# A transformer block on one core: the second quad's queries between the first maxima, the max rows ahead of the third landing, biases in other periods, and pair 61's averages in another PSUM bank

## The chip, the cores and the metric

The kernel runs on one core of a Trainium2 chip. The metric is the device time of one execution in microseconds. Engines are called by the names that the profile uses: PE (TensorE, with PEld for its weight loads), DVE (VectorE), ACT (ScalarE), POOL (GpSimd), SP (the engine whose queue issues most of the DMAs). PSUM has eight banks of 128 partitions by 512 fp32 values, numbered 0 to 7 here.

## The reference, cut to what matters

Four batches of 512 tokens with 256 features pass one block: self-attention, cross-attention to a context of 512 rows with 192 features, and an MLP. Both attentions have 16 heads of 64 features with rotary positions.

```python
attn_in = _adaln(x, cond, ln1_w, ln1_b, g1_w, g1_b, b1_w, b1_b)
x = _attn(attn_in, attn_in, sa_wq, sa_wkv, sa_wo, sa_bo) + x
cross_in = _adaln(x, cond, ln1_w, ln1_b, g1_w, g1_b, b1_w, b1_b)
ctx_n = _ln(context, ca_lnc_w, ca_lnc_b)
x = _attn(cross_in, ctx_n, ca_wq, ca_wkv, ca_wo, ca_bo) + x
ffn_in = _adaln(x, cond, ln2_w, ln2_b, g2_w, g2_b, b2_w, b2_b)
h = jax.nn.gelu(ffn_in @ ff_w1 + ff_b1, approximate=False)
x = h @ ff_w2 + ff_b2 + x
```

`_attn` projects q, k and v, rotates q and k, takes softmax(q k^T / 8), averages v with it and projects the result with `wo`, plus a bias `bo`.

## The kernel before

**Precision.** Each fp32 operand of a large matmul is split into a high part (rounded) and a low part (the rest), and three products are summed: high by high, high by low, low by high (`parts`, L712). The high parts are made on ACT, the low parts by a subtraction on DVE or POOL (`low_qk` L1081, `low_o` L1077, `norm_split` L288, `low_weights` L296, `split_ffw` L1112).

**Units of work.** A pair is two heads of one batch, one in each half of the 128 partitions; there are 64 pairs (`PAIRS`), numbered g. Two neighbouring pairs are a quad (32 of them, `QUADS`, numbered u), which share weights and projections. A job j is one projection for a quad: job 2u gives the keys and job 2u+1 the queries (`k = 1 - j % 2`). A job's two halves e come out of PE (`project`), are multiplied with the rotation table on DVE (`rotate` L1086), added up on POOL (`rotate` L422) and moved by two DMAs of SP into `lo` (`land` L338). ACT rounds them into `hi` (`high_qk`), DVE subtracts (`low_qk`).

**The loop.** After a hand-written head, every engine runs `period(p)` for p = 0 to 63, in its own order, and then a tail with the MLP. In period p PE does, alternating, `score(p, i)` and `peak(p+1, i)` for i = 0 to 3, then `total(p-1)`, `average(p, kt)`, a norm's transposes if one is due, `project(p+4)`, and in every second period v's projection or the output projection. A peak is a trial product of high parts, from which DVE takes the negated maxima (`peak` L1061, `neg_max`); SP brings these as rows into `max_rows` (`land_max` L347), and `score` adds them through a matmul with `pick` before ACT takes the exponential (`exp`). POOL adds the four blocks of probabilities in three additions of 128x1024 (`add_probs`), which `total` sums over partitions. ACT and DVE make the inverse of that sum (`guess_inverse`, `normalise`), and DVE scales the average with it.

**What orders the work around the change.**

- Each engine does its instructions in program order and waits on counting semaphores. SP's queue is in order too.
- The head on PE ends with `peak(0, 0..3)`, `norm(2, ..)` and `project(3)`, the queries of quad 1. Each half of `project(3)` waits for a half of job 2's rotation, and its second half for maximum 2 of pair 0.
- `score(g, 0)` waits for `qk_low`, `max_landed`, `av_kept` (ACT has copied the last averages out of bank 1) and `o_low`. The scores use banks 0 to 3, the peaks banks 4 to 7. `peak(p+1, 0)` waits for both halves of job p+3's rotation on DVE (`roped`), and `peak(g, i)` for i above 1 waits for the maximum two before it.
- `peak(p+1, 0)` and `(.., 1)` also wait in `side_free` for the output projection's two sums, which DVE adds to x (`add_out` L1102) at the end of an even period.
- `sum_ps(60)` is bank 4, `sum_ps(63)` bank 6, all others bank 0. Averages are in bank 1.
- `low_qk` for pair 1 is on DVE in period 0. `low_qk(p+2)` comes before the rotation in most periods, and after it where DVE takes a norm's statistics (`stats_in`: periods 0, 5, 9, 13, 17 and some later ones).
- POOL adds the attention's output bias to x (`add_bias`, one 128x1024 addition per batch) in periods 0, 1, 5 and 7 for the first sublayer.
- In the tail, `hidden(f)` is the MLP's first matmul for block f. Block 0 uses bank 3 and block 1 bank 0, so `hidden(1)` waits for `o_low` 63, the `low_o` of pair 62.

## Time and profile before

| what | value |
|---|---|
| time, median of 3 runs | 1118.84 us (1118.40 to 1119.14) |
| the profiled execution's own time | 1118.88 us |
| its span | 1117.1 us, 18312 instructions |
| PE busy | 1097.2 us, 98% of the span |
| DVE busy | 858.1 us, 77% |
| POOL busy | 775.7 us, 69% |
| ACT busy | 636.9 us, 57% |
| mean granted PE clock | 0.994 of full |

The times of rows are us from the start of the span. A line of the timeline gives start, duration, engine, line of the kernel, operation, output and inputs, and in brackets the idle time of the engine before it and what ended that. Matmuls overlap, so a matmul's own duration is longer than the distance to the next. In a line with several instructions (x2, x4) the duration reaches from the first's start to the last's end.

### The profile page before, as it was taken

To read this page: it belongs to the slowest core of one execution; us is meant where nothing else is said; L and a number is where in the kernel's file an instruction comes from. 1 tells how busy PE (TensorE), PEld (TensorE's weight loads), DVE (VectorE), ACT (ScalarE), POOL (GpSimd) and SP (SyncE) were. 2 spreads that over 40 slices of the span, in tenths; PEclk is the share of its full clock that TensorE was granted. 3 is DMA by queue.
4 is the path that set the end of the run, shared out by engine and by line. 5 is a ranking of instruction groups with operands and counts; after the bars stand their busy time and mean duration, and the time that the engine had idled before them with its cause. 6 is when DMAs were issued, how large, how long until landed. Compare 5 with 4: busy or idle time off the path is not lost.

```text
span 1117.1 us, 18312 instructions
## 1 busy us (share of the span) xinstructions
PE 1097.2 (98%) x6904; PEld 785.1 (70%) x6904; DVE 858.1 (77%) x1023; ACT 636.9 (57%) x895; POOL 775.7 (69%) x503
## 2 busy tenths in 40 slices
PE   8989999999999999999999999999999999989998
PEld 7657666776666776666766667766666776756997
DVE  5878887878787777878888777777877777788554
ACT  6465565665666555577665555555555545775521
POOL 2687887787788767789799766777777667755210
PEclk9899999999999999999999999999999999999999
DMA  6312121311231111211121112211121111300001
GB/s 175 86 46 57 32 53 39 89 30 30 53 77 38 39 36 23 72 39 39 29 63 38 39 39 59 51 23 36 38 72 39 37 31 30 114 1 1 20 19 38
DMA packets 59606, 52.31 MB, mean 47 GB/s; under 512 B 23040, under 2 KB 42496, under 8 KB 59264
## 3 DMA queue, kind: packets, MB, share of 16 engines
q1 hardware_dynamic: 57632, 49.57, 18.5%
q10 hardware_dynamic: 1888, 1.59, 0.5%
q8 instruction: 55, 0.90, 0.3%
q14 instruction: 31, 0.25, 0.1%
HBM read 15.22 MB, written 2.10 MB: 16 GB/s over the span
## 4 chain that ended last, share of the span: by engine, by line
PE 90%; DVE 5%; ACT 2%; issue 1%; DMA 1%; SPq 0%; POOL 0%; ACTq 0%; POOLq 0%; DVEq 0%
PE ps L872 18%; PE ps L713 12%; PE ps L715 11%; PE ps L714 11%; PE ps L813 6%; PE ps L860 6%; PE ps L848 5%; PE ps L819 5%; PE ps L815 5%; PE ps L817 5%; PE ps L963 4%; DVE lo L1083 1%; PE ps L729 1%; DMA x<-x_dram 1%; DVE w_lo L1117 1%
## 5 line engine op out<-in xcount | busy, mean ns | idle before, releaser
L548 ACT ACTIVATE probs<-ps 128x1024 f32<-128x1024 f32 x256 | 262.5, 1027 | 208.0 <-PE ps L819 183.6
L1065 DVE TENSOR_REDUCE neg_max<-ps 128x2 f32<-128x1024 f32 x256 | 301.6, 1226 | 76.7 <-PE ps L848 76.7
L420 POOL TENSOR_TENSOR acc<-acc,probs 128x1024 f32<-128x1024 f32 x128 | 306.2, 2392 | 18.6 <-POOL acc L415 0.4
L872 PE MATMUL ps<-probs,v 128*64 128x512 f32 x1024 | 230.7, 592 | 0.0
L415 POOL TENSOR_TENSOR acc<-probs 128x1024 f32<-128x1024 f32 x64 | 153.2, 2394 | 72.1 <-ACT probs L548 72.1
L872 PEld LDWEIGHTS ps<-probs,v 128*64 128x64 f32 x1024 | 73.9, 137 | 146.1 <-issue 146.1
L429 POOL TENSOR_TENSOR eo<-tmp 128x512 f32<-128x512 f32 x63 | 89.7, 1424 | 120.2 <-DVE tmp L1092 120.1
L1092 DVE TENSOR_TENSOR tmp<-ps,rope 128x1024 f32<-128x1024 f32 x126 | 148.2, 1211 | 4.5 <-PE ps L715 4.3
L813 PE MATMUL ps<-max_rows,pick 64*128 64x512 f32 x512 | 109.3, 419 | 2.6 <-DVE o_lo L1079 1.6
L713 PE MATMUL ps<-xn_hi,w_hi 128*128 128x512 f32 x256 | 107.8, 421 | 2.5 <-DVE o_lo L1079 1.3
L848 PE MATMUL ps<-hi 64*128 64x512 f32 x512 | 104.8, 400 | 5.4 <-DVE neg_max L1065 2.6
L819 PE MATMUL ps<-hi,lo 64*128 64x512 f32 x512 | 104.0, 396 | 0.0
L715 PE MATMUL ps<-xn_hi,w_lo 128*128 128x512 f32 x256 | 102.8, 402 | 0.0
L815 PE MATMUL ps<-hi 64*128 64x512 f32 x512 | 102.7, 392 | 0.0
L817 PE MATMUL ps<-lo,hi 64*128 64x512 f32 x512 | 102.4, 390 | 0.0
L714 PE MATMUL ps<-xn_lo,w_hi 128*128 128x512 f32 x256 | 102.0, 398 | 0.0
L1083 DVE TENSOR_TENSOR lo<-lo,hi 128x1024 fp32r<-128x1024 f32 x64 | 98.3, 1535 | 0.0
L1070 DVE SCALAR_TENSOR_TENSOR ps<-ps,inv 128x512 f32<-128x512 f32 x64 | 44.8, 700 | 68.6 <-ACT inv L556 68.6
L580 ACT COPY v<-ps 128x512 f32<-128x512 f32 x64 | 37.4, 589 | 100.5 <-PE ps L715 100.5
L848 PEld LDWEIGHTS ps<-hi 64*128 64x128 f32 x512 | 81.0, 306 | 17.8 <-issue 5.2
L430 POOL TENSOR_TENSOR eo<-tmp 128x512 f32<-128x512 f32 x63 | 81.3, 1291 | 0.0
L713 PEld LDWEIGHTS ps<-xn_hi,w_hi 128*128 128x128 f32 x256 | 49.0, 192 | 45.4 <-issue 33.9
(116 smaller groups left out, 2250.0 us busy)
## 6 DMA issues: line engine op xcount, KB each, us to landing
lo<-eo SPq DMA_DIRECT2D x126, 256.0 KB, 3.2
w_raw<-pack_dram SPq DMA_DIRECT2D x16, 192.0 KB, 3.9
x<-x_dram SPq DMA_DIRECT2D x4, 512.0 KB, 7.5
w_raw<-pack_dram SPq DMA_DIRECT2D x8, 256.0 KB, 4.3
max_rows<-neg_max SPq DMA_DIRECT2D x128, 2.0 KB, 2.0
w_raw<-w_dram SPq DMA_DIRECT2D x2, 1024.0 KB, 5.8
out<-x SPq DMA_DIRECT2D x8, 256.0 KB, 2.2
ctx_in<-ctx_dram SPq DMA_DIRECT2D x4, 384.0 KB, 4.2
```

The lines of the kernel that those rows point to most:

```text
L420: pool.tensor_tensor(acc[:, g % 2, :, :], acc[:, g % 2, :, :], probs[:, i, :, :], ALU.add).then_inc(added, 1)
L548: act.activation(probs[:, i, :, :], score_ps(i), ACT.Exp, scale=SCALE).then_inc(exped, 1)
L713: pe.matmul(out, a_hi, b_hi, start=first, stop=False)
L714: pe.matmul(out, a_hi, b_lo, start=False, stop=False)
L715: return pe.matmul(out, a_lo, b_hi, start=False, stop=last)
L813: pe.matmul(out[:, h, :], pick[half[h], :], max_rows[half[h], :], start=True, stop=False)
L815: pe.matmul(out[:, h, :], k_hi[half[h], cut], q_hi[half[h], :], start=False, stop=False)
L817: pe.matmul(out[:, h, :], k_hi[half[h], cut], q_lo[half[h], :], start=False, stop=False)
L819: mm = pe.matmul(out[:, h, :], k_lo[half[h], cut], q_hi[half[h], :], start=False, stop=True)
L848: mm = pe.matmul(out[:, h, :], hi[half, g % 2, 0, cut], hi[half, g % 2, 1, :], start=True, stop=True)
L872: mm = pe.matmul(av_ps[DH * h:DH * h + DH, :], v[:, u % 2, kt, c:c + DH], probs[:, kt, h, :], start=(kt == 0), stop=(kt == TT - 1))
L1065: dve.tensor_reduce(neg_max[:, g % 2, :, i], peak_ps(i), AX.X, ALU.max, negate=True).then_inc(maxed, 1)
```

## The change

- **Head, PE.** `project(3)` is cut in four steps of three matmuls, `project_3(e, kt)`: (0,0) before `peak(0, 2)`, (0,1) before `peak(0, 3)`, (1,0) and (1,1) after it, all before `norm(2, ..)`. The waits for job 2's rotation are left out, that for maximum 2 stays.
- **Head, SP.** `land_max(0)` comes ahead of `land(2)`.
- **Head, ACT and POOL.** `high_qk(1)` comes ahead of `guess_rstd(2)`. The low parts of pair 1 are made on POOL after `rotate(3)`, with a semaphore of their own, and no more on DVE in period 0. DVE has nothing then between the maxima of pair 1 and the statistics of norm 3.
- **Biases.** The first sublayer's four `add_bias` go to periods 13, 15, 18 and 21 and wait for the output projection of quad 4 + b; `add_out` no longer waits for them in that sublayer's first two rounds.
- **Pair 61.** Its averages go to bank 5. `score(62, 0)` then waits neither for `av_kept` nor for `o_low`; `peak(63, 0)` waits for both.
- **Periods 61 to 63, DVE.** In period 61 the statistics of norm 13 come ahead of `normalise(60)`, and their means ahead of `low_o(60)`. `split_ffw` is one subtraction of 128x2048 instead of four of 128x512, twice. In period 63 DVE adds probability blocks 2 and 3 of pair 63 into `tmp`, POOL only blocks 0 and 1, and `total(63)` sums both with four matmuls instead of two.

```diff
-        av_ps = ps[:, 1, :]
+        def av_ps(g):
+            return ps[:, 5 if g == PAIRS - 3 else 1, :]
...
-        bias_in.update({0: 0, 1: 1, 5: 2, 7: 3})
+        bias_in.update({13: 0, 15: 1, 18: 2, 21: 3})
...
             land(1)
+            land_max(0)
             land(2)
-            land_max(0)
             load_x(3)
...
                 pool.wait_ge(ln_rows, TT * (n + 1))
+                if sublayer == 0:
+                    pool.wait_ge(o_added, 2 * (NB + b) + 2)
...
                     add_probs(p, 1)
-                    add_probs(p, 2)
-                    add_probs(p, 3)
+                    if p < PAIRS - 1:
+                        add_probs(p, 2)
+                        add_probs(p, 3)
...
             rotate(3)
+            pool.wait_ge(qk_high, 2)
+            pool.tensor_tensor(lo[:, 1, :, :], raw_qk[:, 1, :, :], hi[:, 1, :, :], ALU.subtract).then_inc(qk_low_1, 1)
...
             high_qk(0)
+            high_qk(1)
             guess_rstd(2)
-            high_qk(1)
             norm_rows(2)
...
+            def project_3(e, kt):
+                if e == 0 and kt == 0:
+                    pe.wait_ge(w_split, 2)
+                    pe.wait_ge(ln_split, 4)
+                if e == 1 and kt == 0:
+                    pe.wait_ge(maxed, 3)
+                c = slice(kt * 256 + e * 128, kt * 256 + (e + 1) * 128)
+                mm = parts(job_ps(3, e), w_hi[:, 0, c], w_lo[:, 0, c], xn_hi[:, 1, kt, :], xn_lo[:, 1, kt, :],
+                           kt == 0, kt == 1)
+                if kt == 1:
                     mm.then_inc(projected, 1)
...
                 if kt == 0:
-                    pe.wait_ge(qk_low, g + 1)
+                    if g == 1:
+                        pe.wait_ge(qk_low_1, 1)
+                    else:
+                        pe.wait_ge(qk_low, max(g, 1))
                     pe.wait_ge(max_landed, 32 * (g + 1))
-                    if g > 0:
+                    if g > 0 and g != PAIRS - 2:
                         pe.wait_ge(av_kept, g)
-                    if g > 1:
+                    if g > 1 and g != PAIRS - 2:
                         pe.wait_ge(o_low, g - 1)
...
                     if i == 0 and p == PAIRS - 2:
                         pe.wait_ge(o_low, PAIRS - 3)
+                        pe.wait_ge(av_kept, PAIRS - 2)
...
             def total(g):
-                pe.wait_ge(added, 3 * g + 3)
+                pe.wait_ge(added, 3 * g + (3 if g < PAIRS - 1 else 1))
...
                     pe.wait_ge(o_added, 2 * (QUADS - 1))
+                    pe.wait_ge(last_added, 1)
                 for h in range(2):
-                    mm = pe.matmul(sum_ps(g)[DH * h:DH * h + DH, :], ones[:, :], acc[:, g % 2, h, :], start=True, stop=True)
+                    out = sum_ps(g)[DH * h:DH * h + DH, :]
+                    mm = pe.matmul(out, ones[:, :], acc[:, g % 2, h, :], start=True, stop=g < PAIRS - 1)
+                    if g == PAIRS - 1:
+                        mm = pe.matmul(out, ones[:, :], tmp[:, 0, h, :], start=False, stop=True)
...
             modulate(3)
+            project_3(0, 0)
             peak(0, 2)
+            project_3(0, 1)
             peak(0, 3)
+            project_3(1, 0)
+            project_3(1, 1)
             norm(2, 0)
             norm(2, 1)
-            project(3)
...
             def add_out(u, r):
                 _, b, phase = quad(u)
-                if r == 0:
+                if r == 0 and u >= 2 * NB:
...
+            def split_ffw(m):
+                dve.wait_ge(ffw_high, 4 * m + 4)
                 high, low, raw = ((w1_hi, w1_lo, w1_raw), (w2_hi, w2_lo, w2_raw))[m]
...
+                dve.tensor_tensor(low[:, :, :], raw[:, :, :], high[:, :, :], ALU.subtract).then_inc(ffw_split, 1)
+
+            def add_last_probs():
+                dve.wait_ge(exped, 4 * PAIRS)
+                dve.tensor_tensor(tmp[:, 0, :, :], probs[:, 2, :, :], probs[:, 3, :, :], ALU.add).then_inc(last_added, 1)
...
-                if p == 0:
-                    low_qk(1)
+                if p == PAIRS - 3:
+                    norm_stats(stats_in[p])
                 if is_pair(p - 1):
                     normalise(p - 1)
-                if p in stats_in and p != PAIRS - 3:
-                    norm_stats(stats_in[p])
+                if p == PAIRS - 1:
+                    add_last_probs()
+                if p in stats_in:
+                    if p != PAIRS - 3:
+                        norm_stats(stats_in[p])
                     norm_means(stats_in[p])
                 if is_pair(p - 1):
                     low_o(p - 1)
-                if p == PAIRS - 3:
-                    norm_stats(stats_in[p])
-                    norm_means(stats_in[p])
                 if p == PAIRS - 2:
-                    for c in range(4):
-                        split_ffw(0, c)
+                    split_ffw(0)
```

## Rows read from the trace of the kernel before

**Rows 1.** Windows: stretch, busy us of each engine, PEclk, DMA share, GB/s.

```profile
36.00:43.00 7.00, 6.31 (x20) 5.25 (x20) 4.53 (x11) 3.43 (x6) 3.56 (x3) 0.53 0.47 113
...
105.00:980.00 875.00, 874.14 (x5595) 611.45 (x5595) 689.53 (x767) 515.29 (x708) 666.44 (x405) 1.00 0.20 46
...
1019.00:1022.00 3.00, 3.00 (x8) 2.33 (x8) 2.70 (x5) 2.71 (x5) 2.83 (x4) 0.50 0.01 3
```

**Rows 2.** Timeline of TensorE in the head and periods 0 and 1.

```profile
36.69 1.97 PE L729 MATMUL ps<-ident,z 128*128 128x128 f32 x8 [1.40 <-ACT z L505]
...
58.02 0.62 PE L848 MATMUL ps<-hi 64*128 64x512 f32 x2 [1.54 <-DVE tmp L1092]
...
62.43 0.63 PE L848 MATMUL ps<-hi 64*128 64x512 f32 x2 [1.70 <-DVE neg_max L1065]
...
64.99 1.80 PE L860 MATMUL ps<-acc,ones 128*64 128x512 f32 x4
```

**Rows 3.** Timeline of VectorE in the head and periods 0 and 1.

```profile
32.26 4.61 DVE L1065 TENSOR_REDUCE neg_max<-ps 128x2 f32<-128x1024 f32 x4
...
43.34 1.22 DVE L1092 TENSOR_TENSOR tmp<-ps,rope 128x1024 f32<-128x1024 f32 x1 [0.86 <-PE ps L715]
...
49.96 3.38 DVE L1083 TENSOR_TENSOR lo<-lo,hi 128x1024 fp32r<-128x1024 f32 x1
...
57.80 3.43 DVE L1083 TENSOR_TENSOR lo<-lo,hi 128x1024 fp32r<-128x1024 f32 x1
```

**Rows 4.** Timeline of GpSimd over the same stretch.

```profile
40.22 2.63 POOL L293 TENSOR_TENSOR xn_lo<-z,xn_hi 128x512 fp32r<-128x512 f32 x2 [3.24 <-ACT xn_hi L520]
...
45.90 1.29 POOL L430 TENSOR_TENSOR eo<-tmp 128x512 f32<-128x512 f32 x1
...
49.89 5.70 POOL L420 TENSOR_TENSOR acc<-acc,probs 128x1024 f32<-128x1024 f32 x2
...
57.77 2.39 POOL L437 TENSOR_TENSOR x<-x,bias_rows 128x1024 f32<-128x1024 f32 x1
```

**Rows 5.** Timeline of SyncE: DMA issues behind pair 0's maxima.

```profile
37.01 1.17 SPq L345 DMA_DIRECT2D lo<-eo  x2
38.30 1.77 SPq L354 DMA_DIRECT2D max_rows<-neg_max  x2
```

**Rows 6.** DMA issues of the page: size, median us from issue to landing.

```profile
lo<-eo SPq DMA_DIRECT2D x126, 256.0 KB, 3.2
...
max_rows<-neg_max SPq DMA_DIRECT2D x128, 2.0 KB, 2.0
```

**Rows 7.** Timeline of period 18 and its end: GpSimd, VectorE, TensorE.

```profile
328.59 4.91 POOL L420 TENSOR_TENSOR acc<-acc,probs 128x1024 f32<-128x1024 f32 x2
...
333.61 1.21 DVE L1083 TENSOR_TENSOR lo<-lo,hi 128x1024 fp32r<-128x1024 f32 x1
...
337.01 1.37 DVE L1109 TENSOR_TENSOR x<-ps,x 128x512 f32<-128x512 f32 x2
...
338.60 0.41 PE L848 MATMUL ps<-hi 64*128 64x512 f32 x2
```

**Rows 8.** Timeline of TensorE in period 3, behind its first score.

```profile
93.25 0.62 PE L848 MATMUL ps<-hi 64*128 64x512 f32 x2 [0.20 <-DVE x L1109]
```

**Rows 9.** Timeline of TensorE in periods 62 and 63 and the tail.

```profile
989.46 0.50 PE L813 MATMUL ps<-max_rows,pick 64*128 64x512 f32 x2 [1.55 <-DVE o_lo L1079]
...
995.26 1.08 PE L860 MATMUL ps<-acc,ones 128*64 128x512 f32 x4
...
1018.19 0.51 PE L713 MATMUL ps<-xn_hi,w_hi 128*128 128x512 f32 x1 [1.27 <-DVE o_lo L1079]
```

**Rows 10.** Timeline of VectorE and ScalarE in the same stretch.

```profile
989.23 1.40 DVE L1050 BATCH_NORM_STATS2 stats<-x 128x6 f32<-128x256 f32 x4
...
1004.90 8.64 DVE L1117 TENSOR_TENSOR w_lo<-w_raw,w_hi 128x512 fp32r<-128x512 f32 x4
...
1010.85 0.63 ACT L556 ACTIVATE inv<-inv 128x512 f32<-128x512 f32 x1
```

More of the change, by code:

```diff
@@ L742, in project @@
                 for e in range(2):
[L743 to L746 removed]
+                    if j == 1:
+                        pe.wait_ge(roped, e + 1)
                     for kt in range(KT):
@@ L1150, in period @@
                 if p == PAIRS - 2:
-                    for c in range(4):
-                        split_ffw(1, c)
+                    split_ffw(1)
             norm_stats(0)
```

21 lines of the change are left out of this document (7 added, 14 removed).

## The prediction, made before the change was run

> **What bounds the kernel.** I read the windows first, then the list of what TensorE waited for, then the timelines of the two places where it waits, and last the DMA issues. Between 105 and 980 us PE is busy for 874.1 of 875 us at full clock [rows 1], so nothing off PE can be worth a microsecond there. PE's idle time lies in the head with periods 0 and 1, and from period 60 on, and there it is a chain over the other engines that counts. In the head the reader should see three things: PE waits 1.40 us for the normalised rows and then runs at a granted clock of 0.53 from 36 to 43 us [rows 1, 2]; PE waits twice in period 1, 1.54 us for DVE's rotation and 1.70 us for a maximum [rows 2]; and before both waits DVE has a subtraction of 3.4 us in its queue [rows 3]. In the tail PE waits 1.55 us at 989.46 and 1.27 us at 1018.19, each time for a `low_o` of DVE [rows 9].
>
> **Why 3.4 us.** The same subtraction took 1.21 us in period 18 [rows 7]. The one at 57.80 began 0.03 us behind POOL's bias addition, which ended at 60.16; 1.07 us later DVE was done [rows 3, 4]. The one at 49.96 stands beside additions of POOL in the same way. So a DVE operation with both inputs in SBUF that comes behind a POOL operation waits for its end, then takes its own 1.1 to 1.2 us, and POOL's next one waits in turn.
>
> The Trainium skill ("SBUF — State Buffer", Who interferes with whom) says this as a rule: DVE with two SBUF inputs and a GpSimd instruction that reads SBUF share a port under an exclusive lock, and the second to issue blocks until the first is done. By that rule, the trace agrees: 3.43 us beside 1.21.
>
> **Head, step by step.** Pair 0's four maxima fill 32.26 to 36.87 on DVE, 1.15 us each [rows 3], so maximum 2 is there at 35.7. `project_3`'s first half (two steps of about 0.7 us at full clock) fits between the peaks without delaying a maximum. Its second half starts at 35.75 and ends at 37.2. `norm(2)` then starts 0.5 us later than its 36.69 [rows 2], and gives that back if the clock has stayed up (its eight transposes took 1.97 us at half clock).
>
> DVE ends the maxima at 36.87, then has `low_qk(0)` and `modulate(1)`, 2.5 us, then both halves of rotation 3 at 1.22 us each: 41.8 instead of 44.56 [rows 3]. POOL can't begin `rotate(3)` at 41.8, though. Its two splits of norm 2 ended at 42.85 [rows 4], and I put them between 42.4 and 43.4. `land(2)` is now behind `land_max(0)`: that one is issued at 36.95 and 37.5, its landing (2.0 us [rows 6]) is 39.5, and `land(2)` moves from 37.01 to 38.1 [rows 5], second half 38.7, landed with the usual 3.2 us at 41.9 and with 3.6 at 42.3 [rows 6]. So `rotate(3)` begins at 42.6, bounds 42.4 and 43.4, instead of 44.64.
>
> From there POOL is one chain: rotation 2.55 us to 45.15 (before: to 47.19 [rows 4]), the new subtraction of pair 1 at POOL's 2.4 us for 128x1024 [rows 4] to 47.6, and three additions at 2.4 us to 54.9. That is 0.7 us earlier than the 55.59 of before [rows 4], in spite of one more operation.
>
> The Trainium skill ("GPSIMD Engine Reference", Engine selection) speaks against this move: elementwise work on two inputs belongs on VectorE, GpSimd being about twice as slow. Here the rows are 2.39 against 1.21 us, so the move would cost 1.2 us of engine time; what it buys is that DVE loses 3.38 us.
>
> DVE meanwhile: the maxima of pair 1 begin when `peak(1, 0)` may run, at 41.85, and end at about 47.1. Norm 3's statistics follow at once. Rotation 4 is limited by PE's `project(4)` and ends at 53.2 instead of 57.88, so the wait of 1.54 us goes. Then `low_qk(2)` meets POOL's third addition, waits until 54.9, ends at 56.05; the first maximum of pair 2 is there at 57.2, and `peak(2, 2)` can start then. Before, it was 62.43 [rows 2]: 5.2 us earlier, and PE still waits there, about 1.4 us. From `peak(2, 2)` to `total(0)` it took 2.56 us and the sum's four matmuls 1.80 us [rows 2]; those four take 1.08 at full clock [rows 9]. With full clock `total(0)` is at 58.7, 6.3 us earlier; with a clock that falls again after the waits, 4.7 us. I can't tell which, since PE still has gaps of 1.3, 1.0 and 1.4 us in 38 to 57 us. **Term: -5.6 us**, bounds -6.3 and -3.9 (low clock and `rotate(3)` at 43.4). A low clock earlier, in period 0, costs nothing: POOL's chain does not wait for PE. `high_qk(1)` ahead of `guess_rstd(2)` fills 1.8 us in which ACT waits for the variances anyway: 0.
>
> **Biases.** Those of periods 0 and 1 were 2.4 us each in POOL's queue; period 0's is the one that held `low_qk(2)`, counted above. Without period 1's, POOL and DVE are earlier before period 3, where PE waited 0.20 us [rows 8]: -0.2 (0 to -0.5). Period 13 has the same neighbours as 5 (a norm's statistics, a weight split in the next period), 15 the same as 7; what they cost moves with them: 0, within 0.5 either way. Period 18 is different. It is even, with `add_out` at its end. POOL's additions end at 333.50 and the bias would start there; `low_qk` comes at 333.61 [rows 7]. It then waits 2.3 us and ends at 337.0 instead of 334.82. The first `add_out`, done at 337.7 before, comes to 339.9, and the peak that needs it started at 338.60 [rows 7]. **Term: +1.3 us**, bounds 0 (if DVE is first, by 0.1 us) and +2.2. Period 21 is odd: no `add_out`, 0.
>
> **Pair 61 and the statistics.** `score(62, 0)` loses its wait and starts at 987.9. `peak(63, 0)` then waits for `low_o(60)`, which ends where the statistics began, at 989.25 [rows 10]. The statistics now fill DVE's idle time before `normalise(60)`, so `low_qk(63)` (1.2 us) comes at once and the maxima of pair 63 start at 990.4. The first is there at 991.6, `peak(63, 2)` follows, and with one more score and peak `total(61)` starts at 993.15 instead of 995.26 [rows 9]. **Term: -2.1 us**, bounds -1.1 (the start of `peak(63, 0)` alone) and -2.3. All up to `total(62)` hangs on it.
>
> **Last splits.** The four subtractions at 1004.90 took 8.64 us beside POOL [rows 10]. One of 128x2048 takes about 2.3 us plus at most one POOL operation (1.3 us): DVE is free at 1006.5, and `normalise(62)` waits only for the inverse, 1011.48 [rows 10] less 2.1, so 1009.4, instead of 1013.5. Then come 2.2 us of `normalise`, 1.2 of the new addition, 1.4 of statistics [rows 10], 0.6 of means, 0.7 of `low_o`: `hidden(1)` can start at 1015.5 instead of 1018.19 [rows 9]. `total(63)` no longer waits for POOL; its two extra matmuls are in PE's wait before `hidden(1)`, 1.4 us long. **Term: -0.6 us** beyond the 2.1, bounds 0 and -0.9.
>
> **Clock in the tail.** From 1019 to 1022 the clock was 0.50 after two waits of PE close together [rows 1, 9]. It lost 1.5 us there. Now there is one wait. At 989.46 one wait of 1.55 us was not followed by a low clock. **Term: -0.8 us**, bounds 0 and -1.4 (then DVE's first hidden split holds PE). Behind it PE has no wait, so all of this reaches the end.
>
> **Sum.** -5.6 -0.2 +1.3 -2.1 -0.6 -0.8 = -8.0 us, from the profiled execution's 1118.88, which is the median of the runs to 0.04 us: 1110.9.
>
> **Rivals.**
> - *Late chain and low clock in the head* (POOL's splits end at 43.4, PE's clock falls after 57 us): head -3.9, no gain of clock in the tail, the rest as above: -5.5, 1113.4. For it: PE's gaps. Against: fewer of them than before. Chance 0.22.
> - *All terms at their good end*: DVE first in period 18, full clock: 1108.2. For it: a margin of 0.1 us. Chance 0.15.
> - *Biases block everywhere*: the 2.2 us of period 18 at the other three as well: +6.6, 1117.5, which is no change. Against: periods 5 and 7 had a bias and PE lost under 1 us in all of 105 to 980 [rows 1]. Chance 0.05.
> - *Slower*: after the shift POOL's third addition runs later against DVE, so that `low_qk` is held in every even period as before period 3. Its price there was 0.2 us of waiting [rows 8] and, by my estimate, 0.27 to fill the pipeline again; over 30 even periods 0.47 each is 14 us: 1125. It decides from 22 periods on. Against: POOL waits for DVE's rotation in each period and is set right by that. Chance 0.04.
>
> **Chances.** Forecast 0.50 (own range 1109.5 to 1112.5); rivals as given; 0.04 for other sums that are faster. A measurement of this kernel tells about 0.2%, 2.2 us, from no change. Faster 0.91, same 0.05, slower 0.04. The range 1108.4 to 1114.6 leaves out those two, a part of the good end and of the bad clock.
>
> **What the profile after would show.** `rotate(3)` of POOL starting at 42.6 and pair 1's subtraction at 45.2; `low_qk(2)` ending at 56; `peak(2, 2)` near 57.2 with a wait of 1.4 us; `total(0)` between 58.7 and 60.3; a wait of PE in period 19 of 1.3 us; `total(61)` 2.1 us sooner after `total(60)`; `hidden(1)` 2.7 us sooner, with one wait before it. The prediction is wrong if `land(2)` lands after 44 us, if `rotate(3)` waits for it, or if PE has new waits in the middle.

## The result and the profile after

The changed kernel took 1112.12 us in the median of 4 runs (1110.40 to 1112.95), the kernel before 1118.99 us in the same comparison (4 runs, 1118.40 to 1119.45). The ratio is 0.9937, 95% interval 0.9920 to 0.9954: faster by 0.6%. 1110.9 was forecast, in a range of 1108.4 to 1114.6. The profiled execution took 1110.40 us, with a span of 1108.6 us.

The page of the changed kernel (span, busy time of each engine with its share and its instructions):

```profile
span 1108.6 us, 18301 instructions
...
PE 1091.2 (98%) x6908; PEld 779.6 (70%) x6908; DVE 851.0 (77%) x1017; ACT 636.2 (57%) x895; POOL 775.2 (70%) x502
```

Windows of the changed kernel, with the columns of [rows 1]: the head, the middle, the end of the chain in the tail.

```profile
36.00:43.00 7.00, 4.57 (x32) 3.61 (x32) 6.17 (x13) 4.21 (x6) 3.63 (x4) 1.00 0.43 105
105.00:980.00 875.00, 872.80 (x5567) 608.79 (x5567) 690.95 (x769) 514.75 (x707) 670.07 (x405) 1.00 0.20 45
...
1012.00:1022.00 10.00, 9.87 (x64) 8.63 (x63) 9.11 (x15) 6.70 (x11) 5.02 (x4) 1.00 0.00 1
```

The granted clock, 0.53 in 36 to 43 us and 0.50 in 1019 to 1022 us before [rows 1], is 1.00 in both places. In the middle PE now idles 2.2 us instead of 0.9; 1.14 us of it is the wait at the end of period 18.

Timeline of TensorE in the head, answering to [rows 2]:

```profile
39.75 0.50 PE L836 MATMUL ps<-max_rows,pick 64*128 64x512 f32 x2 [1.55 <-DMA max_rows<-neg_max]
...
53.92 0.63 PE L872 MATMUL ps<-hi 64*128 64x512 f32 x2 [0.28 <-DVE tmp L1123]
...
57.30 0.62 PE L872 MATMUL ps<-hi 64*128 64x512 f32 x2 [0.66 <-DVE neg_max L1096]
...
59.03 1.08 PE L886 MATMUL ps<-acc,ones 128*64 128x512 f32 x4
```

Timeline of GpSimd and VectorE in the same stretch, answering to [rows 3, 4]: rotation 3, pair 1's subtraction, pair 0's three additions, the epsilon of norm 3 (`var_eps`), `low_qk(2)`.

```profile
42.73 1.30 POOL L433 TENSOR_TENSOR eo<-tmp 128x512 f32<-128x512 f32 x1 [0.35 <-DMA lo<-eo]
...
45.23 2.38 POOL L478 TENSOR_TENSOR lo<-lo,hi 128x1024 fp32r<-128x1024 f32 x1
...
47.55 2.38 POOL L419 TENSOR_TENSOR acc<-probs 128x1024 f32<-128x1024 f32 x1
...
48.95 1.02 DVE L1090 TENSOR_SCALAR var_eps<-mean_var 128x4 f32<-128x4 f32 x1
...
50.08 4.95 POOL L424 TENSOR_TENSOR acc<-acc,probs 128x1024 f32<-128x1024 f32 x2
...
53.69 2.43 DVE L1114 TENSOR_TENSOR lo<-lo,hi 128x1024 fp32r<-128x1024 f32 x1
```

The chain is the one forecast: POOL from `rotate(3)` on, `low_qk(2)` held until POOL's last addition ends at 55.03, then the first maximum, then `peak(2, 2)`. The line to notice is `var_eps`, an operation on 128x4 values. It takes 0.17 us when POOL is idle; here it takes 1.02 us, and ends 0.04 us behind POOL's addition (47.55 + 2.38 = 49.93). In this execution it costs nothing, for DVE waits for PE behind it.

Timeline of period 18 and its end, answering to [rows 7]:

```profile
325.98 2.40 POOL L443 TENSOR_TENSOR x<-x,bias_rows 128x1024 f32<-128x1024 f32 x1
...
326.16 3.30 DVE L1114 TENSOR_TENSOR lo<-lo,hi 128x1024 fp32r<-128x1024 f32 x1
...
331.65 1.27 DVE L1140 TENSOR_TENSOR x<-ps,x 128x512 f32<-128x512 f32 x2
...
332.47 0.62 PE L872 MATMUL ps<-hi 64*128 64x512 f32 x2 [1.14 <-DVE x L1140]
```

Timeline of periods 61 to 63, answering to [rows 9, 10]:

```profile
983.14 0.87 DVE L1090 TENSOR_SCALAR var_eps<-mean_var 128x4 f32<-128x4 f32 x1
...
983.92 0.68 DVE L1110 TENSOR_TENSOR o_lo<-ps,o_hi 128x512 fp32r<-128x512 f32 x1
...
984.70 0.63 PE L872 MATMUL ps<-hi 64*128 64x512 f32 x2 [0.81 <-DVE o_lo L1110]
...
988.75 1.08 PE L886 MATMUL ps<-acc,ones 128*64 128x512 f32 x4
...
1010.86 0.50 PE L722 MATMUL ps<-xn_hi,w_hi 128*128 128x512 f32 x1 [0.29 <-DVE o_lo L1110]
```

Here the same small operation does cost: it stands ahead of `low_o(60)` in DVE's queue, and it waits for POOL's addition, which ends at 983.98 (the two additions of pair 60 began at 979.09 and filled 4.89 us).

**Where the time went.** The table compares the starts of some matmuls of PE in the two profiles; `total(g)` stands for the first of its matmuls. `down(0)` is the first matmul of the second hidden layer; behind it PE has no wait.

| stretch | before | after | difference | forecast |
|---|---|---|---|---|
| start to `total(0)` | 64.99 | 59.03 | -5.96 | -5.6 |
| to `total(2)` | 32.33 | 30.99 | -1.34 | -0.2 |
| to `total(60)` | 886.07 | 888.23 | +2.16 | +1.3 |
| to `total(61)` | 11.87 | 10.50 | -1.37 | -2.1 |
| to `hidden(1)` | 22.93 | 22.11 | -0.82 | -0.6 |
| to `down(0)` | 5.85 | 4.60 | -1.25 | -0.8 |
| to the end | 93.06 | 93.14 | +0.08 | 0 |
| span | 1117.1 | 1108.6 | -8.5 | -8.0 |

**The spread of the runs.** The executions of one kernel differ by more than some of these rows. The kernel before took 1118.4 to 1119.5 us in all four executions of the first comparison. In later comparisons its executions lay in two heaps: of the 23 of the last comparison 18 took 1114.3 to 1116.0 us and 5 took 1119.1 to 1119.3 us. The changed kernel, run again, took 1112.42 us (7 runs, 1110.6 to 1115.8) beside 1115.70 of the kernel before, ratio 0.9965 (0.9949 to 0.9981). In the other comparisons some executions also lay at 1117.3 to 1118.9 us. So the table speaks for an execution of the upper heap; against the lower heap, as in the second comparison, the change is worth some 3 us. The experiments below come from four later comparisons. Their medians alone can seldom tell a microsecond; their traces can.

### The profile page after: what moved, and what is told of

Read it like the earlier page. It is cut to its first block, busy times and chain, and to the rows that moved or that the text cites. A ratio compares the mean times of both kernels' runs of the same rounds, so it can differ in the third digit from the quotient of the medians.

```text
span 1108.6 us, 18301 instructions
## 1 busy us (share of the span) xinstructions
PE 1091.2 (98%) x6908; PEld 779.6 (70%) x6908; DVE 851.0 (77%) x1017; ACT 636.2 (57%) x895; POOL 775.2 (70%) x502
## 4 chain that ended last, share of the span: by engine, by line
PE 91%; DVE 3%; ACT 2%; issue 1%; DMA 1%; POOL 1%; SPq 0%; ACTq 0%; POOLq 0%
PE ps L900 18%; PE ps L722 12%; PE ps L723 11%; PE ps L724 11%; PE ps L836 6%; PE ps L886 6%; PE ps L872 6%; PE ps L842 5%; PE ps L838 5%; PE ps L840 5%; PE ps L994 4%; PE ps L738 1%; DMA x<-x_dram 1%; DVE lo L1114 1%; DVE neg_max L1096 1%
## 5 line engine op out<-in xcount | busy, mean ns | idle before, releaser
L424 POOL TENSOR_TENSOR acc<-acc,probs 128x1024 f32<-128x1024 f32 x126 | 301.1, 2390 | 18.1
L1114 DVE TENSOR_TENSOR lo<-lo,hi 128x1024 fp32r<-128x1024 f32 x63 | 94.3, 1497 | 0.0
```

What stands on the lines that cost most here:

```text
L424: pool.tensor_tensor(acc[:, g % 2, :, :], acc[:, g % 2, :, :], probs[:, i, :, :], ALU.add).then_inc(added, 1)
```

## The experiments

### The changed kernel and the kernel before, once more

`after_again` is the changed kernel, `before_again` the kernel before; neither has an edit.

> The changed kernel itself, beside the others of this call. Theory 1: faster than the kernel before by 5 to 7 us in the median; the runs spread over some 2.5 us, because the clock falls at one place or another between 8 and 60 us, and a fall behind the maxima of period 0 costs 0.3 us at total(0), one in period 2 over 1 us. Rival: the gain is the same within 0.3 us in each run, and total(0) is at 59.0 us again.

> The kernel before, unchanged, profiled once more. Its executions on this chip lie in two heaps, near 1115.1 and near 1118.6 us, on the first chip at 1118.4 to 1119.5. Theory (the two heaps are one program with PE's clock low at different places of the head and the tail): if this execution is of the lower heap, total(0) starts 2 to 4 us before the 64.99 us of the first profile, with the clock low for less of 32 to 66 us, distances between totals from period 4 on agree within 0.1 us, and the rest of the difference is the tail's low clock in 1019 to 1022 us. If it is of the upper heap, all milestones agree with the first profile within 0.5 us. Rival (the middle differs: another pace of the periods, or of the DMA landings): total(0) agrees and the distances from period 4 on differ by 0.05 us or more each.

`after_again`: `total(0)` at 59.82 us and `total(2)` at 91.87 instead of 59.03 and 90.02. From `total(2)` to the end it took 1018.5 us against 1018.6. All of the 1.8 us between the two profiles of one kernel lie in the first 92 us. In 40 to 48 us the granted clock was 0.79 there instead of 1.00.

`before_again`: its profiled execution was of the upper heap (1119.13 us, span 1117.3), and the milestones agree with the first profile within 0.3 us (64.93, 97.27, 983.65, 995.52; the clock 0.50 in 36 to 40 us again). The ratio to the kernel before is 1.0001 (0.9986 to 1.0016), which is what this measurement makes of no change at all. No execution of the lower heap was profiled. The mean granted clock of the executions doesn't tell the heaps apart: in this comparison it was 0.991 to 0.994 in the upper one and 0.992 to 0.997 in the lower one. Whether the place of the low clock does is neither shown nor refuted.

### The biases back in periods 0, 1, 5 and 7

```diff
-        bias_in.update({13: 0, 15: 1, 18: 2, 21: 3})
+        bias_in.update({0: 0, 1: 1, 5: 2, 7: 3})
...
-                if sublayer == 0:
-                    pool.wait_ge(o_added, 2 * (NB + b) + 2)
...
-                if r == 0 and u >= 2 * NB:
+                if r == 0:
```

> All of the change, but the first sublayer's biases stay in periods 0, 1, 5 and 7. Theory 1 (my steps): the wait of 1.14 us in front of period 19's second peak goes and period 17-to-18's sum distance falls from 16.54 to 15.0 us; total(0) stays near 59.0 us, since low_qk(2) is behind POOL's third addition, ahead of the bias; period 1's bias gives back 0.6 us before period 3. Sum: 1 us faster than the changed kernel, 0.9 either way. Rival (the biases in periods 0 and 1 were what held the head): total(0) comes 2 us later and the whole is 1 to 3 us slower than the changed kernel.

Time 1111.42 us (6 runs, 1109.8 to 1113.2), ratio 0.9947 (0.9930 to 0.9964). `total(0)` came at 61.96, and not because of the bias. Timeline of GpSimd, VectorE and TensorE:

```profile
55.71 3.35 DVE L1112 TENSOR_TENSOR lo<-lo,hi 128x1024 fp32r<-128x1024 f32 x1
...
60.25 0.63 PE L870 MATMUL ps<-hi 64*128 64x512 f32 x2 [1.60 <-DVE neg_max L1094]
...
60.51 2.39 POOL L441 TENSOR_TENSOR x<-x,bias_rows 128x1024 f32<-128x1024 f32 x1
```

The bias runs at 60.51, behind the subtraction and the peak that it was said to hold. What made the head late is the clock, 0.50 in 36 to 40 us in this execution: POOL's rotation 3 began at 45.70 instead of 42.73, 2.97 us later, and `total(0)` 2.93 us later. In the new order of the head it is POOL's last addition that holds `low_qk(2)`, so moving the bias out of period 0 brings nothing at `total(0)`. From `total(0)` to `total(2)`, where period 1's bias is, it took 32.02 us and after the change 30.99. This need not be the bias: two executions of the changed kernel differ there by as much (30.99 and 32.05 us).

Elsewhere the biases did what was forecast, and a swap costs nothing: the distance from `total(5)` to `total(6)` is 15.90 with the bias in 5 and 15.49 without, from `total(13)` to `total(14)` 15.51 and 15.87. From `total(17)` to `total(18)` it is 15.02 with no bias in period 18 and 16.54 with one.

### The third bias in period 19

```diff
-        bias_in.update({13: 0, 15: 1, 18: 2, 21: 3})
+        bias_in.update({13: 0, 15: 1, 19: 2, 21: 3})
```

> All of the change, but the third batch's bias is added in period 19 instead of 18. Theory 1: low_qk of period 18 no longer stands behind the bias, the 1.14 us wait of PE goes and the distance of the sums falls from 16.54 to 15.0 us: 1.5 us faster than the changed kernel, nothing lost in period 19, whose low_qk comes before POOL's bias. Rival: POOL has additions, a weight split, the bias and a rotation in period 19, 14.7 us of a period of 15.1, and falls behind, so that the wait comes one period later with 0.5 us or more.

Time 1110.47 us (6 runs, 1108.8 to 1112.9) beside 1112.42 of the changed kernel in the same comparison; ratios 0.9946 (0.9929 to 0.9963) and 0.9965. The intervals overlap; the trace decides. Timeline of period 18 and of the bias in period 19:

```profile
326.29 1.22 DVE L1114 TENSOR_TENSOR lo<-lo,hi 128x1024 fp32r<-128x1024 f32 x1
...
329.68 1.38 DVE L1140 TENSOR_TENSOR x<-ps,x 128x512 f32<-128x512 f32 x2
...
343.52 2.40 POOL L443 TENSOR_TENSOR x<-x,bias_rows 128x1024 f32<-128x1024 f32 x1
```

The subtraction takes 1.22 us instead of 3.30, `add_out` begins 2 us sooner, and PE's wait is gone. `total(17)` to `total(18)` is 15.05 again, and `total(19)` to `total(20)` 15.31 instead of 15.05. From `total(2)` to `total(60)` it took 886.80 us, 1.4 less than after the change. The `low_qk` of period 19 began at 340.98, before the bias. Two kernels below have this edit too, with medians of 1110.24 and 1110.36 us. The three can't be told apart; their medians are the lowest of all.

### Pair 61's averages and the statistics as before

```diff
-            return ps[:, 5 if g == PAIRS - 3 else 1, :]
+            return ps[:, 1, :]
...
-                    if g > 0 and g != PAIRS - 2:
+                    if g > 0:
...
-                if p == PAIRS - 3:
-                    norm_stats(stats_in[p])
...
                     low_o(p - 1)
+                if p == PAIRS - 3:
+                    norm_stats(stats_in[p])
+                    norm_means(stats_in[p])
```

> All of the change, but pair 61's averages in bank 1 with the old waits of score(62), and norm 13's statistics and means behind low_o(60) as before. Theory 1: total(60) to total(61) goes back from 10.50 to 11.87 us, so 1.4 us slower than the changed kernel and nothing else moves. Rival (the tail is held by low parts and splits further on, so that this time is given back there): hidden(1) starts at the same distance from total(60) and the end moves by less than 0.4 us.

Time 1113.48 us (10 runs, 1112.3 to 1115.1), ratio 0.9969 (0.9958 to 0.9981), in one comparison with `bias_back` at 1111.42. From `total(60)` to `total(61)` it took 11.88 us, before 11.87, after 10.50. Timeline of VectorE and TensorE in period 61:

```profile
984.91 0.69 DVE L1110 TENSOR_TENSOR o_lo<-ps,o_hi 128x512 fp32r<-128x512 f32 x1 [0.65 <-ACT o_hi L583]
985.52 1.39 DVE L1081 BATCH_NORM_STATS2 stats<-x 128x6 f32<-128x256 f32 x4
...
985.75 0.50 PE L836 MATMUL ps<-max_rows,pick 64*128 64x512 f32 x2 [1.55 <-DVE o_lo L1110]
```

That is the wait of [rows 9] at its old length: taken out of the change, this part costs 1.38 us. The next experiment says why it isn't 2.1.

### Norm 13's means behind `low_o(60)`

The bias is in 19 here too.

```diff
-                if p in stats_in:
-                    if p != PAIRS - 3:
-                        norm_stats(stats_in[p])
+                if p in stats_in and p != PAIRS - 3:
+                    norm_stats(stats_in[p])
                     norm_means(stats_in[p])
...
                     low_o(p - 1)
+                if p == PAIRS - 3:
+                    norm_means(stats_in[p])
```

> The third bias in period 19 as before, and norm 13's aggregation and epsilon (128x2 and 128x4) behind low_o(60) instead of ahead of it. Theory (the part of the pair-61 term that did not come is the 128x4 operation of DVE, held 0.87 us behind POOL's addition, with low_o(60) behind it): low_o(60) can start at the end of ACT's o_hi, 4.2 us after total(60)'s four matmuls have ended instead of 4.6, so peak(63, 0) starts 0.4 to 0.5 us sooner after total(60), 6.0 instead of 6.45, and total(61) comes 0.3 to 0.5 us sooner, 10.0 to 10.2 us after total(60) instead of 10.50. Rival (ACT's exponential of (62, 0) stands behind the square root that needs the moved epsilon, and sets the pace then): peak(63, 0) sooner by as much, but the exponential of (62, 0) 0.5 us later, and total(61) 10.4 to 10.8 us after total(60). A third theory (what holds peak(63, 0) is not the lock): peak(63, 0) unmoved. The whole against the kernel with the bias in 19 alone: -0.4 us, within what a timing can tell: about 1110.

Time 1110.24 us (6 runs, 1109.4 to 1111.1), ratio 0.9948 (0.9932 to 0.9965). Timeline of period 61, all engines:

```profile
983.59 0.69 DVE L1110 TENSOR_TENSOR o_lo<-ps,o_hi 128x512 fp32r<-128x512 f32 x1 [0.65 <-ACT o_hi L583]
...
984.38 0.63 PE L872 MATMUL ps<-hi 64*128 64x512 f32 x2 [0.38 <-DVE o_lo L1110]
...
984.61 0.17 DVE L1090 TENSOR_SCALAR var_eps<-mean_var 128x4 f32<-128x4 f32 x1
...
985.16 1.92 ACT L557 ACTIVATE probs<-ps 128x1024 f32<-128x1024 f32 x2
...
986.21 0.19 PEld L836 LDWEIGHTS ps<-max_rows,pick 64*128 64x128 f32 x2 [0.35 <-ACT probs L557]
```

`low_o(60)` starts as soon as ACT has made its input. The epsilon takes 0.17 us, since POOL's addition ended at 984.08. `peak(63, 0)` starts 6.01 us after `total(60)` (978.37) instead of 6.45: the small operation held it for 0.44 us. `total(61)` gains 0.05 us of that (10.45 instead of 10.50), for ACT's square root waits for the moved epsilon, the exponential of (62, 0) starts 6.79 us after `total(60)` instead of 6.14, and PE waits for it. The rival was right: with the small operation no longer in front of `low_o(60)`, the stretch is bound by ACT.

### The last splits in four pieces again

```diff
-                dve.wait_ge(ffw_high, 4 * m + 4)
-                dve.tensor_tensor(low[:, :, :], raw[:, :, :], high[:, :, :], ALU.subtract).then_inc(ffw_split, 1)
...
+                for c in range(4):
+                    cut = slice(c * N, (c + 1) * N)
+                    dve.wait_ge(ffw_high, 4 * m + c + 1)
+                    dve.tensor_tensor(flat[1][:, cut], flat[2][:, cut], flat[0][:, cut], ALU.subtract)\
+                       .then_inc(ffw_split, 1)
```

> All of the change, but the MLP weights' low parts are four subtractions of 128x512 each time, as before. Theory 1: they alternate with POOL's operations and end near 1006 us instead of 1001.4, so normalise(62) starts up to 1 us behind its inverse, hidden(1) comes up to 1 us later and the end as much. Rival (POOL has so much less in period 63 that four pieces fit as well): normalise(62) starts with its inverse at the same distance from total(62), and the time is the same within 0.3 us.

Time 1111.61 us (5 runs, 1110.4 to 1113.1), ratio 0.9955 (0.9938 to 0.9973). Timeline of VectorE:

```profile
998.85 6.47 DVE L1149 TENSOR_TENSOR w_lo<-w_raw,w_hi 128x512 fp32r<-128x512 f32 x4
1005.45 0.70 DVE L1101 SCALAR_TENSOR_TENSOR ps<-ps,inv 128x512 f32<-128x512 f32 x1
```

The four pieces take 6.47 us (one piece took 3.00 in the changed kernel), and still end 0.13 us before `normalise(62)`, for which ACT's inverse is ready then. From `total(61)` to `hidden(1)` it took 22.10 us, in the changed kernel 22.11, and the rest of the span agrees as well. The rival was right. Making one subtraction of the four brings nothing, given the other edits.

### Pair 63's additions on POOL again

```diff
-                    if p < PAIRS - 1:
-                        add_probs(p, 2)
-                        add_probs(p, 3)
+                    add_probs(p, 2)
+                    add_probs(p, 3)
...
-                    if g == PAIRS - 1:
-                        mm = pe.matmul(out, ones[:, :], tmp[:, 0, h, :], start=False, stop=True)
...
-                if p == PAIRS - 1:
-                    add_last_probs()
```

> All of the change, but the last pair's blocks 2 and 3 are added on POOL again, and total(63) has two matmuls. Theory 1: total(63) waits for POOL's third addition until 1.2 us after hidden(0), but low_o(62) is 1.1 us sooner, so hidden(1) starts at the same distance from total(62) within 0.3 us; the end moves by less than 0.5 us unless the clock falls behind the two waits, which then costs 1.3 us. Rival (the move of the addition is what took the tail's second wait away): hidden(1) 1 us or more later.

Time 1112.65 us (7 runs, 1112.0 to 1113.8), ratio 0.9966 (0.9953 to 0.9979). Timeline of VectorE and TensorE:

```profile
1010.75 0.98 DVE L1086 TENSOR_SCALAR var_eps<-mean_var 128x4 f32<-128x4 f32 x1
1011.64 0.68 DVE L1106 TENSOR_TENSOR o_lo<-ps,o_hi 128x512 fp32r<-128x512 f32 x1
...
1011.76 1.08 PE L884 MATMUL ps<-acc,ones 128*64 128x512 f32 x4 [1.22 <-POOL acc L424]
```

`total(63)` comes 7.34 us after `total(62)` instead of 6.03. Most of that is given back, since there are two matmuls less and the addition is gone from DVE's queue: `hidden(1)` comes 22.19 us after `total(61)` instead of 22.11. From there to `down(0)` it takes 4.94 us instead of 4.60, with a wait of 0.48 us for the first hidden split. So this part is worth 0.4 us, 0.1 ahead of `hidden(1)` and 0.3 behind it. Here, too, the small operation is held until POOL's addition ends, with a `low_o` behind it.

### Pair 1's subtraction on DVE again

```diff
-            pool.wait_ge(qk_high, 2)
-            pool.tensor_tensor(lo[:, 1, :, :], raw_qk[:, 1, :, :], hi[:, 1, :, :], ALU.subtract).then_inc(qk_low_1, 1)
...
+                if p == 0:
+                    dve.wait_ge(qk_high, 2)
+                    dve.tensor_tensor(lo[:, 1, :, :], raw_qk[:, 1, :, :], hi[:, 1, :, :], ALU.subtract)\
+                       .then_inc(qk_low_1, 1)
```

This was run once with the bias in 18 (`low1_on_dve`) and once with it in 19 (`low1_bias19`).

> All of the change, but pair 1's low parts are subtracted on DVE in period 0 again, not on POOL. Theory 1: POOL's chain starts its additions 2.4 us sooner (45.2), the third ends near 53.6 with one wait for DVE; DVE's subtraction costs 1.2 to 1.7 us that lie in its wait for project(4); low_qk(2) starts at 53.7 free of POOL, so peak(2, 2) is near 56.1 instead of 57.3: the move to POOL brings nothing or costs 1 us, and the gain of the head is project_3's alone. Rival (the move off DVE is the head's gain, as the prediction's text weighs it: DVE loses 3.4 us): rotation 4 and the maxima of pair 2 are late again, total(0) is 2 to 3 us later and the kernel as much slower than the changed one.

> Pair 1's subtraction on DVE again, ahead of low_qk(2) in period 0, and the third bias in period 19. Theory (a subtraction of DVE that stands alone costs DVE 1.2 us, and POOL's chain of rotation, subtraction and three additions loses 2.4 us of its length, but DVE's subtraction falls beside an addition and is held to its end, so that nothing is won): total(0) at 60.1 to 60.4 us with the clock falling after 42 us, 59.0 to 59.6 without; behind period 0 all distances as with the bias in 19. Time 1110.5 to 1111.5. Rival (POOL's shorter chain is worth what the prediction took from its length, 1.2 us or more): total(0) at 58 us or sooner, time 1109.5 or less.

Times 1112.56 us (6 runs), ratio 0.9959 (0.9944 to 0.9973), and 1110.36 us (6 runs, 1109.5 to 1112.7), ratio 0.9954 (0.9936 to 0.9972). Timeline of the first, GpSimd and VectorE:

```profile
47.97 5.71 POOL L424 TENSOR_TENSOR acc<-acc,probs 128x1024 f32<-128x1024 f32 x2
...
48.95 2.47 DVE L1157 TENSOR_TENSOR lo<-lo,hi 128x1024 fp32r<-128x1024 f32 x1
```

DVE's subtraction is held to the end of an addition and takes 2.47 us; POOL's next addition waits in turn, so that POOL loses 0.8 us of the 2.4 that it saves (5.71 for two additions instead of 4.9). `total(0)` came at 60.15 and 61.48 us, but the clock was low in both, the second at 0.65 already in 32 to 36 us, ahead of the edit. So neither can be laid beside the changed kernel's first profile. The first of them can be laid beside the four profiles that have the subtraction on POOL and the same clock, 0.79 in 40 to 48 us: their `total(0)` is at 59.30 to 59.84, 0.3 to 0.9 us sooner. But its `total(2)`, at 91.14, is sooner than theirs (91.46 to 91.87), and the second median, 1110.36, is close to 1110.24, that of the kernel with the means behind, in the same comparison. Whether the move to POOL gains anything in the time stays open.

### `project_3` behind the peaks, and the rows behind the third landing

```diff
-            project_3(0, 0)
             peak(0, 2)
-            project_3(0, 1)
             peak(0, 3)
-            project_3(1, 0)
-            project_3(1, 1)
             norm(2, 0)
             norm(2, 1)
+            project_3(0, 0)
+            project_3(0, 1)
+            project_3(1, 0)
+            project_3(1, 1)
```

```diff
-            land_max(0)
             land(2)
+            land_max(0)
```

> All of the change, but project_3's four steps stand behind norm(2) as before. Theory 1: rotation 3 ends on DVE at 44.6 again, POOL's rotate(3) runs at 44.6 instead of 42.7 and its chain with the new subtraction ends 1.9 us later, so total(0) is 2 us later, and 1 to 2 us more if the clock falls as it did from 36 to 43 us: 2 to 4 us slower than the changed kernel. Rival (the queue of DVE and POOL in period 0 sets total(0) whatever the projection does): less than 1 us slower.

> The rows of maxima are again issued behind the third landing; the rest is the changed kernel. The part alone. Theory (the head is POOL's chain from rotate(3) on, which waits for this landing): land(2) is issued at 37.0 instead of 38.26, so rotate(3) of POOL starts when its own splits have ended, 42.4 us, 0.35 sooner; score(0, 0) waits for the rows, which land at 40.5 to 41 instead of 39.6, so it starts 1.2 us later; the maxima of pair 1 begin up to 1 us later, and total(0) is within 0.4 us of 59.0 where the clock is the same. Rival (score(0, 0) sets the head): total(0) 1 us or more later. Clock rival: PE's longer wait ahead of score(0, 0) brings a low clock in 36 to 48 us, and total(0) comes at 60 or later.

`project3_behind`: 1112.23 us (5 runs), ratio 0.9958 (0.9943 to 0.9973). PE waits again for the normalised rows and its clock falls to 0.50 in 36 to 40 us, as before the change; DVE's rotation 3 begins at 41.74 us instead of 39.36, and the chain follows it:

```profile
37.18 1.97 PE L738 MATMUL ps<-ident,z 128*128 128x128 f32 x8 [1.24 <-ACT z L514]
...
44.76 1.29 POOL L433 TENSOR_TENSOR eo<-tmp 128x512 f32<-128x512 f32 x1 [1.42 <-DVE tmp L1123]
```

`rotate(3)` at 44.76 instead of 42.73 and `total(0)` at 61.05 instead of 59.03: both 2.0 us later. By the profiles this is the largest single part of the head, the low clock included. The timed runs don't show it: 1112.23 us is no more than the 1112.42 of the changed kernel in another comparison.

`maxrows_behind`: 1111.53 us (7 runs, 1110.6 to 1111.8), ratio 0.9957 (0.9940 to 0.9973), in one comparison with two kernels of 1110.3 that have the bias in 19. The landing no longer holds POOL, and PE waits 3.39 us for the rows:

```profile
41.57 0.50 PE L836 MATMUL ps<-max_rows,pick 64*128 64x512 f32 x2 [3.39 <-DMA max_rows<-neg_max]
...
42.32 1.29 POOL L433 TENSOR_TENSOR eo<-tmp 128x512 f32<-128x512 f32 x1
```

`rotate(3)` is 0.4 us sooner, `score(0, 0)` 1.8 us later, the clock falls to 0.86 in 40 to 44 us and 0.71 in 44 to 48 us, and `total(0)` comes at 60.09, 1.06 us later. POOL's chain is not what made it late, for its last addition ends 0.45 us sooner than after the change, and `low_qk(2)` (55.80) takes 1.22 us, unheld: it stands behind rotation 4, and that behind PE. These are the clock rival's numbers. How much of it is the clock and how much the later `score(0, 0)` isn't separated.

## Why the forecast came out right, and what it had wrong

**Head, -5.6, measured -5.96: right step by step in the profiled execution, but for two.** `rotate(3)` was put at 42.6 us and came at 42.73, but for another reason than the one forecast. The landing was counted at 41.9 to 42.3, ahead of the end of POOL's splits. The splits ended at 42.37 and POOL then waited 0.35 us for the landing, which the prediction had named as a sign of being wrong. The other is the sum itself: with a low clock `peak(2, 2)` at 57.2 and the old 2.56 us behind it give 59.76, 5.2 us earlier, not 4.7.

The other steps: pair 1's subtraction was put at 45.2 and came at 45.23. `low_qk(2)` ends: 56.05, came at 56.12. `peak(2, 2)`: 57.2, came at 57.30. `total(0)`: 58.7 to 60.3, came at 59.03. One detail was off: PE's wait ahead of `peak(2, 2)` was 0.66 us and not 1.4, because PE itself had waited 0.28 us for rotation 4 and issued `peak(2, 0)` only at 53.92. The rotation of job 4 stood behind the held `var_eps`, but not because of it: it waited 1.18 us more for PE. The clock, said to be unknowable, stayed at 1.00 in this execution.

Of the 5.96 us the reversals above account, by profiles whose clock differs, for 2.0 (`project_3`) and 1.1 (the order of the landings); `high_qk(1)` ahead of `guess_rstd(2)` was not taken back in any run, and how the rest divides isn't shown. In the three profiles with full clock from 32 to 48 us (the changed kernel, the bias in 19, the splits in four) `total(0)` starts at 58.98 to 59.16; in the other four with the same head, all at a lower clock in 40 to 48 us, at 59.30 to 59.84.

**A low clock early in period 0, put at nothing.** "POOL's chain does not wait for PE" is true, but at the low clock another chain is the longer one: PE, pair 1's maxima, norm 3's statistics and epsilon, rotation 4. Timeline of GpSimd and VectorE in the kernel with pair 61 as before, at a clock of 0.68 in 40 to 44 us:

```profile
50.22 4.93 POOL L424 TENSOR_TENSOR acc<-acc,probs 128x1024 f32<-128x1024 f32 x2
...
50.26 2.37 DVE L1090 TENSOR_SCALAR var_eps<-mean_var 128x4 f32<-128x4 f32 x1
52.54 2.54 DVE L1123 TENSOR_TENSOR tmp<-ps,rope 128x1024 f32<-128x1024 f32 x2
55.00 1.23 DVE L1114 TENSOR_TENSOR lo<-lo,hi 128x1024 fp32r<-128x1024 f32 x1
```

The epsilon comes 1.3 us later than in the changed kernel's first profile, meets the next addition of POOL and is held for 2.37 us; rotation 4 follows without a wait, and `low_qk(2)` is not held at all. In two others rotation 4 also waits 0.2 us for PE. In all four profiles `low_qk(2)` takes 1.21 to 1.25 us and starts at 55.00 to 55.56, instead of 53.69, held, for 2.43.

**To `total(2)`, -0.2, measured -1.34: two things were left out.** The first 0.72 us lies between `total(0)` and `total(1)` and is the clock. Before, it was at 0.50 until 66.5 us, past the start of `total(0)`: its four matmuls took 1.80 us [rows 2] and now take 1.08. The prediction quoted both numbers, but measured its gain at the start of `total(0)` and so left the difference out. The other 0.62 us lies between `total(1)` and `total(2)`. The term counted POOL and DVE "earlier before period 3, where PE waited 0.20 us". What happens there is a race of two operations. Timeline of the kernel before, of the changed kernel and of the kernel with the means behind, in period 2:

```profile
87.55 2.69 DVE L1083 TENSOR_TENSOR lo<-lo,hi 128x1024 fp32r<-128x1024 f32 x1
```

```profile
78.39 5.96 POOL L424 TENSOR_TENSOR acc<-acc,probs 128x1024 f32<-128x1024 f32 x2
...
80.87 1.22 DVE L1114 TENSOR_TENSOR lo<-lo,hi 128x1024 fp32r<-128x1024 f32 x1
```

```profile
78.40 4.92 POOL L424 TENSOR_TENSOR acc<-acc,probs 128x1024 f32<-128x1024 f32 x2
...
81.52 2.88 DVE L1114 TENSOR_TENSOR lo<-lo,hi 128x1024 fp32r<-128x1024 f32 x1
...
87.41 0.63 PE L872 MATMUL ps<-hi 64*128 64x512 f32 x2 [0.37 <-DVE x L1140]
```

In the changed kernel, DVE starts 0.05 us ahead of POOL's third addition (80.92) and goes first: 1.22 us, and POOL waits, at no cost. In the third kernel, PE was 0.64 us later in the head; DVE comes inside the third addition, is held, and `add_out` and the peak are late. Before, DVE came inside it too. The distance from `total(1)` to `total(2)` is 15.00 us in the changed kernel, 15.79 in the third and 15.62 before.

All twelve profiles of the changed kernel and its variants fall in with this. Where that subtraction took 1.21 or 1.22 us (four), `total(0)` to `total(2)` took 31.0 us. Where it was held to 2.84 to 3.40 us (five), it took 31.8 to 32.3. Where DVE came so late that it was held to 1.80 to 1.99 us only (three), 31.0 again. That the head's delay picks one of the three cases is read from these starts, not tested by itself. So a low clock in 40 to 48 us costs first its own delay, 0.3 to 0.8 us at `total(0)`, and then, if the delay falls badly, 0.8 to 1.3 us more here. The forecast took the head's clock to be paid for at `total(0)`, and of the race it saw a wait of 0.20 us.

**Middle, +1.3, measured +2.16.** The mechanism was right, with the wait of 1.3 us found at 1.14, and the period is 1.53 us longer. Putting the bias in 19 takes 1.43 us of the stretch back. Period 5 gained 0.43 and period 13 lost 0.40, as forecast. The rest, 0.6 us, lies in the eleven distances from `total(p)` to the next for odd p from 37 to 57: 15.12 us each instead of 15.07. `before_again` has 15.12 there too, so this part is no effect of the change but differs between executions of one kernel; why is not shown.

**Pair 61, -2.1, measured -1.37: the mis-sized term.** The step that failed is "`peak(63, 0)` then waits for `low_o(60)`, which ends where the statistics began". `peak(63, 0)` started 6.45 us after `total(60)` where 5.86 were counted, because the means and the epsilon now stand ahead of `low_o(60)`, and the epsilon waits for POOL: 0.44 us by the experiment. Another 0.15 us is the way from the end of `low_o(60)` to the peak's start: the forecast took the start of DVE's next operation, which is recorded 0.06 us ahead of that end, and the peak starts 0.10 us behind it. The last 0.15 us is PE's own: the forecast let the first maximum set the pace, and PE needs 4.05 us from `peak(63, 0)` to `total(61)` without a wait where 3.90 were counted. That makes 10.50 us instead of 9.76. The forecast knew of the lock for operations with two large inputs only. And the moved means have shown that the lock's 0.44 us was not to be had: ACT's exponential came next, and 0.05 us was won.

The Trainium skill ("SBUF — State Buffer", Who interferes with whom) lists `tensor_scalar`, under conditions, among the operations of DVE that can take both ports and so contend with GpSimd; the trace agrees, with 0.17 us for it beside an idle POOL and 0.52 to 2.37 us beside an operation of POOL, at 128x4 values. The same section says that the order of issue decides who is blocked; by it, period 2 above goes as the trace shows, 1.22 us or 2.88 for one operation.

**Last splits, -0.6, measured -0.82.** The size was right; which of the two edits brings it isn't shown. Taken back alone, the single split costs nothing up to `hidden(1)` and the addition given to DVE 0.08 us. In both cases `normalise(62)` starts as soon as the inverse is ready, so either edit seems to be enough; no run took back both. `hidden(1)` came 2.19 us sooner after `total(60)`, where 2.7 were forecast; pair 61's shortfall of 0.73 is in that.

**Clock in the tail, -0.8, measured -1.25.** With one wait of 0.29 us ahead of `hidden(1)` instead of 0.63 and 1.27 us close together, the granted clock stayed at 1.00. The 1.5 us that the low clock had cost came back, and 0.3 us were lost again: `down(0)` waits for DVE's first hidden split, which ends at 1015.40, 0.06 us ahead of it. The prediction had named this wait. In `last_on_pool` a single wait of 1.22 us stands there, and the clock stayed at 1.00 too; that two waits close together lower it is read from the kernel before, in two profiles, and wasn't tested by itself.

**The sum.** Four gains came out larger than forecast (by 0.36, 1.14, 0.22 and 0.45 us), one smaller (0.73) and the loss larger (0.86): -8.0 forecast, -8.5 in the profiled execution. That these nearly cancel is luck; the head's -5.96 carries the forecast. There is luck in the comparison too: the forecast was made for an execution of the upper heap, and so were all four that the result was compared with. From the lower heap, near 1115 us, the same -8.0 would have given 1107, and no execution of the changed kernel took less than 1110.4. The median of the timed runs is 6.9 us down and not 8.5, because the profiled execution is the fastest of the four, which lie between 1110.4 and 1112.95 us; `after_again` shows a difference of this kind to lie wholly in the head and period 2. Of the rivals, the late chain with the low clock is the one that the other executions came nearest to; of the even periods none but 18 was newly held (the 0.27 us that this rival took for filling the pipeline again were an estimate; behind a wait the rows have 0.43 us from a peak to the next matmul, 58.02 to 58.45, where 0.23 is usual), and the biases in 13 and 15 blocked no more than they had in 5 and 7.

## What to carry to other kernels

Before moving a small DVE operation ahead of one that TensorE waits for, look at what GpSimd runs at that moment: what counted here was not the operation's own 0.17 us, but the rest of GpSimd's instruction. And where two engines block one another, write down the margin between their starts, for a delay of 0.6 us elsewhere flipped the order here and cost another 0.8 us. A job that can go in any of several periods belongs in one without work behind it that TensorE waits for, here an odd one.

## What the runs showed of the hardware that was not expected

A `TENSOR_SCALAR` of DVE on 128x4 values, 0.17 us alone, is held by GpSimd. This isn't rare: the fourteen profiles have 66 such `var_eps`, four to six in each, of 0.52 to 2.37 us. Each of them began beside a 128x1024 operation of GpSimd and ended 0.02 to 0.04 us behind it. The kernel before has four of them, three in its middle (1.03, 0.95 and 1.39 us, at 501, 532 and 564 us), so the prediction could have read this from its trace. The longest of all is the one of 2.37 us shown above, at the low clock in the head.

The kernel before, unchanged, gave two heaps of times some 4 us apart (0.4%) in one comparison. A comparison of a few runs, all of which happen to fall in one heap of the kernel before, can show twice the gain of one that mixes them.
